# One decoder layer on one core: maxima of the cross attention before the later batches' output and norm, a reciprocal root on VectorE, and weight loads in another place

## What is computed

```
x = x + attn(layernorm(x))            # 16 heads of 64; everything rounded to 1/4096
x = x + xattn(layernorm(x), ctx)      # 16 heads of 8, 1601 keys; mask added to the scores
x = x + ffn(layernorm(x))             # 8 experts, the best 2 per token
```

## Time and profile before

| | |
|---|---|
| median of 3 runs | 681.28 us |
| the profiled execution | 678.65 us |
| its span, first to last instruction | 676.9 us |
| mean granted TensorE clock | 0.933 of full |
| TensorE matmul busy | 565.7 us (84%) |
| VectorE busy | 497.0 us (73%) |
| ScalarE busy | 473.9 us (70%) |
| GpSimd busy | 141.0 us (21%) |

### The profile page before, as it was taken

One profiled execution on the slowest core, in us unless ns is written; L12 is line 12 of the kernel. 1 busy time (PEld: TensorE's weight loads), 2 busy tenths in 40 slices (PEclk: granted clock), 3 DMA queues, 4 the chain that ended last, 5 costly groups with the idle time before them and its releaser, 6 DMA issues.

```text
span 676.9 us, 13952 instructions
## 1 busy us (share of the span) xinstructions
PE 565.7 (84%) x5108; PEld 315.7 (47%) x5115; DVE 497.0 (73%) x896; ACT 473.9 (70%) x850; POOL 141.0 (21%) x215
## 2 busy tenths in 40 slices
PE   5799888988869468999889988999896894799992
PEld 3465555555548233333333333333331242799992
DVE  2578889888986977888878888888884433667662
ACT  3879999998983027778678875878674773577760
POOL 5001001000003433230125011500012106232332
PEclk9999999999999759999999999999996877699995
DMA  9822845723768427010641037000005001111103
GB/s 232 246 103 74 167 166 129 197 83 117 205 174 205 76 98 249 2 51 1 144 126 50 2 67 204 2 1 3 1 1 190 2 1 50 40 41 44 42 28 101
DMA packets 31669, 62.89 MB, mean 93 GB/s; under 512 B 4526, under 2 KB 21338, under 8 KB 31156
## 3 DMA queue, kind: packets, MB, share of 16 engines
q0 software_dynamic: 8000, 40.91, 22.9%
q1 hardware_dynamic: 22020, 20.31, 10.2%
q10 hardware_dynamic: 1584, 0.79, 0.4%
HBM read 42.29 MB, written 19.30 MB: 91 GB/s over the span
## 4 chain that ended last, share of the span: by engine, by line
PE 46%; DVE 20%; ACT 16%; DMA 8%; issue 7%; SPq 1%; POOL 0%; POOLq 0%; ACTq 0%; DVEq 0%
DVE smax L1684 13%; PE pair L1099 11%; PE pair L1074 6%; PE pair L1260 6%; ACT region_p L1340 5%; PE pair L1029 5%; PE pair L1248 3%; ACT region_p L1348 3%; ACT region_p L1438 2%; PE pair L929 2%; DMA region_b<-in_mask_Bx1xSxS_ff 2%; PE pair L916 2%; PE pair L900 2%; PE pair L1270 1%; ACT region_p L1326 1%
## 5 line engine op out<-in xcount | busy, mean ns | idle before, releaser
L1684 DVE TENSOR_REDUCE smax<-pair 128x2 f32<-128x1024 f32 x192 | 225.5, 1219 | 53.5 <-PE pair L1029 52.8
L1438 ACT ACTIVATE region_p<-pair 128x1024 f32<-128x1024 f32 (+3 forms) x277 | 217.7, 812 | 66.8 <-PE pair L1074 61.5
L1557 DVE SCALAR_TENSOR_TENSOR region_p<-region_p 128x1024 int16<-128x1024 int16 (+1 forms) x56 | 67.1, 1220 | 10.3 <-ACT region_p L1326 8.2
L1099 PE MATMUL pair<-region_p 128*32 128x256 f32 (+1 forms) x832 | 69.9, 410 | 0.5 <-ACT region_p L1445 0.4
L1099 PE MATMUL pair<-region_p,region_b 128*32 128x256 f32 (+1 forms) x832 | 66.5, 391 | 0.4 <-ACT region_p L1445 0.4
L1074 PE MATMUL pair<-region_b,region_k 59*128 59x256 bf16 (+1 forms) x416 | 54.7, 273 | 8.7 <-ACT region_p L1438 4.3
L1029 PE MATMUL pair<-region_k,region_b 56*128 56x512 bf16 (+1 forms) x256 | 44.3, 364 | 18.7 <-DVE smax L1684 17.5
L1340 ACT ACTIVATE region_p<-region_p 128x256 f32<-128x256 int16 x128 | 51.4, 413 | 0.0
L916 PE MATMUL pair<-ident,region_p 128*128 128x128 f32 x256 | 36.3, 287 | 11.8 <-DVE region_p L1590 11.8
L1260 PE MATMUL pair<-region_p 128*128 128x128 f32 x368 | 45.5, 277 | 0.0
L929 PE MATMUL pair<-region_p 128*64 128x256 f32 x256 | 34.7, 392 | 12.4 <-ACT region_p L1348 11.5
(11 more groups left out here) (244 smaller groups left out, 970.2 us busy)
## 6 DMA issues: line engine op xcount, KB each, us to landing
kimg<-region_k SPq DMA_DIRECT2D x56, 200.1 KB
region_k<-kimg POOLq DMA_DIRECT2D x8, 1400.9 KB, 18.1
region_b<-in_mask_Bx1xSxS_ff POOLq DMA_DIRECT2D x12, 800.5 KB, 7.6
region_p<-in_mask_Bx1xSxS_ff POOLq DMA_DIRECT2D x4, 800.5 KB, 12.9
region_k<-in_L_ffn_W POOLq DMA_DIRECT2D x3, 1024.0 KB, 9.5
xdisp<-region_x POOLq DMA_DIRECT2D x1, 2322.0 KB, 19.0
region_b<-in_ctx SPq DMA_DIRECT2D x3, 768.0 KB
xdisp<-region_x POOLq DMA_DIRECT2D x1, 2257.5 KB, 18.5
```

What stands on the lines that cost most here:

```text
L1099: last = pe.matmul(pair[3][32 * h:32 * h + 32, 512 + s % 2 * S:512 + (s % 2 + 1) * S], v_heads[b % 2][0:rows, t, c:c + 32], pT[0:rows, n / ...
L1438: act.activation(pT[0:rows, first // 3 % 2, k:k + size], home[0:rows, 0:size], ACT.Exp).then_inc(expt_made, 1)
L1557: return dve.scalar_tensor_tensor(out_, floor16, 0.0, floor16, ALU.is_lt, ALU.add)
L1684: last = dve.tensor_reduce(units[:, :, c // 3, c % 3], both, AX.X, ALU.max)
```

## The change

- **Maxima first.** VectorE no longer outputs and norms tiles 2 to 7 ahead of the maxima. `out_move` only evicts them to 16 bit (`later16`), tiles 2 to 5 before the first pair, 6 and 7 before pair 4. The rest is `out_later(piece)`, six pieces behind pairs 19, 21, 23, 25, 27 and 29, for all six tiles together. TensorE projects tiles 2 and 3, transposes batch 0's queries, projects 4 and 5, and then 6 behind pair 1 and 7 behind pair 2.
- **Lead.** 18 pairs run before event 0 instead of 22; two pairs per event follow until the old schedule is met (`pairs_by`).
- **Queries among scores.** Batches 1, 2 and 3 are transposed in events 30, 50 and 70 in the next free slot of the ring of `pair[0]` and `pair[1]`, and ScalarE copies them after the next event's exponential. The pair that takes the slot next waits for the copy.
- **Root.** The later tiles' norm and the one at event 255 take 1/sqrt by iteration on VectorE, 14 dependent instructions (`norm_root`); the first, second and last norm keep ScalarE's root.
- **GpSimd.** It clamps batch 0's mask and splits maxima 0 and 1 ahead of the later queries. `Wg` and `Wl` are loaded after `split_maxima(7)`. `experts_load` also waits until the shift of group 14 has landed.
- **Branch.** The last batch's `finish_tiles` stand in both branches.
- **Flag.** The reduction of the probe follows `make_attn`, its transposition follows `attn_transposes`.

```diff
+def pairs_by(e):
+    return min(FIRST + 2 * (e + 1), LEAD + 3 * (e + 1) // 4)
 def pairs_at(e):
-    return range(LEAD + 3 * e // 4, LEAD + 3 * (e + 1) // 4)
+    return range(pairs_by(e - 1), pairs_by(e))
...
+QUERIES_AT = (30, 50, 70)
-QUERIES_AT = KT + TAIL_AT
+LATER_AT = (19, 21, 23, 25, 27, 29)
...
# GpSimd
+            for t in range(2):
+                mask_clamp(0, t)
+            split_maxima(0)
+            split_maxima(1)
             pool.wait_ge(proj_mm, len(OUT_TILES))
...
-            pool.wait_ge(xn_made, 1 + len(OUT_TILES))
+            pool.wait_ge(xn_made, 3)
...
-            split_maxima(0)
-            pool.wait_ge(x1_made, len(OUT_TILES))
+            pool.wait_ge(x1_made, 2)
             mask_load(1)
...
+            def gates_load():
+                pool.wait_ge(qstack_made, B)
+                for n, w in enumerate((Wg, Wl)):
...
             def experts_load():
+                pool.wait_ge(shift_loaded, 32 * (GROUPS - 1))
...
             for s in range(1, GROUPS):
-                split_maxima(s)
+                if s > 1:
+                    split_maxima(s)
+                if s == 7:
+                    gates_load()
                 if s == GROUPS - 2:
                     experts_load()
# TensorE
+            project_out(1, (2, 4))
             queries_T(0, pair[0])
-            project_out(2)
+            project_out(1, (4, 6))
...
+                for later in range(1, B):
+                    if n == SLOT["queries", later]:
+                        pe.wait_ge(qstack_made, later + 1)
...
-                for p in range(LEAD):
+                for p in range(FIRST):
                     pair_of_chunks(p, masked)
-                    if p == QUERIES_AT:
-                        for b in range(1, B):
-                            queries_T(b, pair[2 + (b + 1) % 2])
-                pe.wait_ge(qstack_made, B)
+                    if p in (1, 2):
+                        project_out(2, (5 + p, 6 + p))
+                pe.wait_ge(out_moved, 2)
                 burst(st_bank[2])
...
+                        if e in QUERIES_AT:
+                            b = QUERIES_AT.index(e) + 1
+                            pe.wait_ge(slot_done, SLOT["queries", b] - 1)
+                            queries_T(b, pair[SLOT["queries", b] % 2])
...
             with pe.If(flag == 0):
                 cross_attention(False)
+                last_finish()
# VectorE
+            def norm_root(tiles):
+                cut_ = slice(*tiles)
+                root, half, square = rstd[:, cut_], std[:, cut_], meanvar[:, cut_, 1]
+                chain.step(dve.tensor_scalar(half, var_eps[:, cut_], -0.5, None, ALU.mult))
+                chain.step(dve.tensor_scalar(root.bitcast(I32), var_eps[:, cut_].bitcast(I32), 1, None, ALU.logical_shift_right))
+                chain.step(dve.tensor_copy(square, root.bitcast(I32)))
+                chain.step(dve.tensor_scalar(square, square, -1.0, ROOT_MAGIC, ALU.mult, ALU.add))
+                chain.step(dve.tensor_copy(root.bitcast(I32), square))
+                for _ in range(3):
+                    chain.step(dve.tensor_tensor(square, root, root, ALU.mult))
+                    chain.step(dve.tensor_tensor(square, square, half, ALU.mult))
+                    chain.step(dve.scalar_tensor_tensor(root, square, 1.5, root, ALU.add, ALU.mult))
...
+            def out_move(c):
+                first, end = OUT_TILES[c]
+                dve.wait_ge(proj_mm, c + 1)
+                dve.scalar_tensor_tensor(later16[:, first - 2:end - 2, :], ...).then_inc(out_moved, 1)
+            def out_later(piece):
+                # 0 truncate, 1 add x, 2 norm_stats, 3 norm_var, 4 norm_root, 5 norm_apply
...
             attention_out(0)
-            attention_out(1)
-            attention_out(2)
+            out_move(1)
...
-            for p in range(LEAD):
+            for p in range(FIRST):
+                if p == 4:
+                    out_move(2)
                 pair_of_chunks(p)
             for e in range(EVENTS):
                 for p in pairs_at(e):
                     pair_of_chunks(p)
+                    if p in LATER_AT:
+                        out_later(LATER_AT.index(p))
...
                 if e == X2_AT:
-                    layer_norm(5, acc, FFN_TILES[0])
+                    norm_stats(acc, FFN_TILES[0])
+                    chain.step(norm_var(FFN_TILES[0]))
+                    norm_root(FFN_TILES[0])
+                    norm_apply(4, acc, FFN_TILES[0])
```

More of the change, by code:

```diff
@@ L62 @@
 REST = S2 - 3 * CHUNK
-LEAD = 22
+LEAD, FIRST = 22, 18
 TAIL_AT = 4
@@ L102, in slot_table @@
 def slot_table():
-    order = []
+    order, table = [], {}
     def pair_of_chunks(p):
@@ L114, in slot_table @@
             pair_of_chunks(p)
+        if e in QUERIES_AT:
+            table["queries", QUERIES_AT.index(e) + 1] = len(order)
         if finish_at(e):
@@ L117, in slot_table @@
     order += [("finish", B - 1, piece) for piece in range(3)]
-    table = {key: n for n, key in enumerate(order)}
+    table.update({key: n for n, key in enumerate(order)})
     for s in range(GROUPS):
@@ L971, in head_pair, with project_out @@
                         pe.transpose(any_row, mask_any[:, :], ident[:, :]).then_inc(any_T, 1)
-                    attn_transposes(hp, b)
                     if last and b == 2:
-                        project_out(0)
-            def project_out(c):
-                first, end = OUT_TILES[c]
-                pe.wait_ge(o_made, B * (HP - 1) + end // 2)
-                for i, t in enumerate(range(first, end)):
+                        project_out(0, OUT_TILES[0])
+            def project_out(c, tiles):
+                pe.wait_ge(o_made, B * (HP - 1) + (tiles[1] + 1) // 2)
+                for t in range(*tiles):
+                    i = t - OUT_TILES[c][0]
                     for n in range(HP):
@@ L983, in project_out @@
                                          wpT[:, n, :], start=(n == 0), stop=(n == HP - 1))
-                last.then_inc(proj_mm, 1)
+                if tiles[1] == OUT_TILES[c][1]:
+                    last.then_inc(proj_mm, 1)
             for hp in range(HP):
@@ L1202, in biases_T, with last_finish @@
                 last.then_inc(bias_rows_T, 1)
[L1204 to L1208 removed]
+            def last_finish():
+                finish_tiles(B - 1, 0, pair[2])
+                finish_tiles(B - 1, 1, pair[3][:, 0:256])
+                biases_T()
+                finish_tiles(B - 1, 2, pair[3][:, 256:512])
+            pe.wait_ge(flag_made, 1)
+            flag = pe.value_load(mask_flag[0:1, :].bitcast(U32))
+            with pe.If(flag == 0):
+                cross_attention(False)
+                last_finish()
+            with pe.Else():
+                cross_attention(True)
+                last_finish()
+            xn_transposes(5, pair[2], FFN_TILES[1])
             gates(1)
@@ L1407, in queries_move @@
                 act.wait_ge(q_T, b + 1)
-                home = pair[2 + (b + 1) % 2 if b else 0]
+                home = pair[SLOT["queries", b] % 2 if b else 0]
                 act.activation(qstack[b], home[:, :].bitcast(BF16).rearrange("p (h q) -> p h q", h=HP), ACT.Copy).then_inc(qstack_made, 1)
@@ L1421, in _ @@
             queries_move(0)
-            std_of(3, OUT_TILES[1])
-            std_of(4, OUT_TILES[2])
-            for b in range(1, B):
-                queries_move(b)
             act.activation(warm[:, :], var_eps[:, 0:1], ACT.Exp)
@@ L1553, in layer_norm @@
                 last.then_inc(xn_made, 1)
+            def layer_norm(n, root, src, tiles=(0, NT), meanwhile=None):
+                norm_stats(src, tiles)
+                norm_var(tiles).then_inc(var_made, 1)
+                if meanwhile:
+                    meanwhile()
+                dve.wait_ge(std_made, root)
+                chain.step(dve.reciprocal(rstd[:, slice(*tiles)], std[:, slice(*tiles)]))
+                norm_apply(n, src, tiles)
             def truncate(out_, floor16):
@@ L1666, in attention_out @@
                 dve.tensor_copy(rows_of(2), xn_0).then_inc(qnat_made[0], 1)
-                for t in range(2):
-                    dve.wait_ge(mask_loaded[t], 16)
-                    dve.tensor_scalar(masks[0][:, t, :], masks[0][:, t, :], LOWEST, None, ALU.max).then_inc(mclamp_made, 1)
+            def out_move(c):
+                first, end = OUT_TILES[c]
+                dve.wait_ge(proj_mm, c + 1)
+                dve.scalar_tensor_tensor(later16[:, first - 2:end - 2, :], out_home[c].rearrange("p (t d) -> p t d", t=end - first),
+                                         NUDGE, bproj_fx[:, :].unsqueeze(1).broadcast_to([128, end - first, D]),
+                                         ALU.mult, ALU.add).then_inc(out_moved, 1)
+            def out_later(piece):
+                tiles = slice(*LATER)
+                if piece == 0:
+                    dve.wait_ge(out_moved, 2)
+                    chain.step(truncate(xn[:, tiles, :], later16))
```

(15 more changed lines are left out.)

60 lines of the change are left out of this document (24 added, 36 removed).

## The result

The changed kernel takes 690.64 us in the median of 20 runs (682.71 to 707.34), the kernel before 680.49 (676.53 to 685.09, 20 runs). The ratio is 1.0099, 95% interval 1.0069 to 1.0128; the comparison leaves the longest runs out, which is why it is under the ratio of the medians, 1.015. The forecast was 684.2 in a range of 672 to 691. The profiled execution takes 684.10 us, span 680.8, where the sum had given 681.55. So two things need explaining: 2.5 us in the profiled execution, and that the median lies 6.5 above it, with a spread of 25 us where the kernel before has 9. Of the 2.5, 1.5 lie outside the span: 3.3 us here against 1.75. In the changed kernel's 20 runs this share is 1.7 to 3.5 us, in 71 runs of the kernel before 1.7 to 1.8; which edit does it, no run shows. Inside the span the sum is short by 1.0: 3.9 us for 2.9.

The account below looks back on a forecast made before the run. DVE was taken to bound the lead, TensorE the cross attention, DVE and ACT close behind. Terms -1.7 + 2.3 + 4.6 - 7.7 + 10.6 - 5.2 = +2.9 gave 681.55 us profiled, 684.2 median; range 672 to 691.

Parts of the forecast that it names:

- second rival: Query transposes among scores cost all they contain, nothing hidden: 6.5 us more than booked, 690.7 us; chance 0.15.
- step 4: Query transposes at events 30, 50, 70: next pair waits for ACT's copy, 1.9 us each; loss 4.6 us.
- step 3: POOL's order: split of maxima 2 comes late behind query split, mask load and clamp; TensorE waits, loss 2.3 us.
- step 1: Lead: first maximum at 220.5, first exponential about 245.7, 13.3 us earlier, not booked as gain.
- 2. Catch-up: DVE's pairs 18 to 29 and six pieces: pair 30 starts at 269.4 instead of 271.11, gain 1.7 us.
- 5. Expert weights: Loads behind shift 14: TensorE's 6.31 us gap and the half clock behind it go, gain 7.7 us.
- 6. Gate weights: Loads ahead of shift 7: shift lands with them, an 8.3 us gap and half clock behind, loss 10.6 us.
- 7. Tail: Last norm, branch and first block: table switch goes, row transfers limit the gain to about 5.2 of 7.6 us.
- first rival: Shift 7 is not held behind the gate weights: without the 10.6 us, 673.6 us; chance 0.19.
- The third: Rival on the lead: the early start counts in full, 11.6 us better, 672.6 us; chance 0.06.

Follow-up runs that it names:

- run 4: Changed kernel with the second batch's first mask clamp moved behind the split of group 2's maxima; 686.43 us.
- run 5: Changed kernel with GpSimd's two clamps of the first batch's masks held until the first queries are split; 687.76 us, ratio to before 1.0105.
- run 2: Changed kernel without the expert-weight loads' wait for the shift of group 14; 706.16 us.
- run 7: Changed kernel with the first batch's clamps held and queries transposed at events 31, 51 and 67 instead of 30, 50 and 70; 682.99 us.
- run 1: Changed kernel with the gate-weight loads also waiting until shift 7 has landed; 676.48 us, ratio to before 0.9916.
- run 10: Kernel before plus expert weights behind shift 14 and the norm at event 255 with its root by iteration; 672.98 us, ratio 0.9816.
- run 9: Changed kernel with first clamps held, and first masks' and second batch's key loads held until the ones have landed; 688.97 us.
- run 3: Kernel before with only the expert-weight loads' wait for shift 14 added; 672.00 us, ratio 0.9883.
- run 8: Changed kernel with the first batch's clamps held and 22 pairs of chunks ahead of the first scores instead of 18; 684.83 us.
- run 6: Kernel before with only the clamps of the first batch's masks moved from VectorE to GpSimd; 680.29 us, ratio 1.0007.
- run 12: Changed kernel with the mends of run 1, run 4, run 7 and run 9 together; 676.80 us, ratio to before 0.9931.

## Why the prediction was right or wrong

A small loss was forecast and a small loss came: 2.9 us forecast, 3.9 inside the span of the profiled execution, and in the median some 6 us more than forecast, 0.4 under the upper end of the range. That the median is the second rival's 690.7 is chance: that rival put 6.5 us more on the query steps, where the profile has 2.1 more. Within the profile, too, errors cancel: steps 1 to 3 came out 2.5 us better (1.1 of it a self attention that ended earlier), steps 5 and 6 together 3.2 better, stretch 5-6 0.4 better; step 4's stretches and the tail came out 4.2 worse, and 2.9 belong to no step. By its steps, in the profiled execution:

1. Lead: first maximum at 218.97 for 220.5, first exponential at 243.72 for 245.7, of which 1.1 is a self attention that ended earlier. It held for this execution only. What failed is the sentence "The clamps of batch 0 cost POOL 8.5 us while it is free" in step 3, and that step 1 took the start of the transposes, "when DVE has them", as a fixed time. In run 4 T0 lay 5 us later by the clamps alone, in run 5 6 by the late ones alone, in run 2 14 by both. That is enough for the longest runs. What lifts the median by 6.5 us over the profile stays open: these delays are of the size, but holding the clamps moved only the longest runs, and two profiles of fourteen have the ones late. I had asked what hides each edit, not which slack before absorbed the DMAs' lateness: the 8.5 us of output and norm that the change took out of the way.
2. Catch-up: pair 30 starts at 267.01 for 269.4; less those 1.1, a gain of 3.0 where 1.7 was forecast, inside its bounds.
3. GpSimd's order: a wait of 2.08 for the split; by run 4 1.9 for it and 0.8 for the half clock behind it, 2.7 for **2.3**. Right, mechanism and size.
4. Queries: 2.43, 2.61 and 2.47 in the stretches 2-3, 3-4 and 4-5, 7.5 in all; less the 0.8 of step 3, 6.7 for **4.6**. The mechanism is right, the term mis-sized: 2.5 each instead of 1.9. The 1.1 that I took off for shift 2 is there once GpSimd is in time: in run 4 the first of the three costs 1.6. Run 7 shows that the next pair's wait isn't what costs, which leaves ScalarE's copy.
5. Expert weights: 9.0 for **7.7**; right.
6. Gate weights: 8.7 for **10.6**. The mechanism is right (run 1), the size by how it is held: the shift did not wait for the transfer to drain, it took 6.82 us as shift 14 had taken 6.99, and the weights flowed on at 352 GB/s from its landing at 392.42 to 395. I had the number in the earlier trace rows and computed another. The Trainium skill (page "DMA: Bandwidth & Descriptors", section "Queues, rings and completion order") says that the engines take turns between the queues packet by packet; the reading of it in the prediction, a delay of near nothing, is refuted: 6.3 to 6.8 us for shift 7 in seven executions, 7.0 to 7.6 for shift 14 in three, 1.8 for either with the wait.
7. Tail: 4.3 at the first block, 3.9 at the end, for **5.2**, inside its bounds; the row transfers do bound it, as the chain of waits and TensorE's first block show:

```profile
576.52 2.29 DMA xdisp<-region_x,slots
...
579.90 1.84 DMA region_p<-xdisp
```
```profile
581.78 0.48 PE L1267 MATMUL pair<-ident,region_p 128*128 128x128 f32 x1 [2.83 <-DMA region_p<-xdisp]
```

I had not separated its parts, and the runs don't either: in run 10, without the branch's edit, nothing of the root's gain arrived, but in run 9, with it, next to nothing did either, both at a clock of about 0.7. In the sum the tail's gain leans on what TensorE's clock does there.

Not in the sum: 2.9 us behind shift 9 (stretch 9-10). It comes without the change's early parts (run 3, 20.83) and stays away with them (run 8, 18.04), so it isn't the change's alone. But a lowered clock stands there in one of five profiles with the old lead and in seven of nine with the new one; whether the change makes it likelier is open.

The first rival (shift 7 not held) falls by run 1, the third (the early start in full) by run 8. The second priced the query steps at 11.1 net, against 6.7 measured.

## What to carry to other kernels

A wait that keeps a bulk load behind one small transfer on the critical path is the cheapest edit here: one line gave 9 us (run 3), and its absence cost 8.7 (run 1). Before taking work out of the space between an uncertain DMA and the critical engine, ask how late that DMA can be, and look at several executions: one profile shows one landing. An engine that is idle is not free if another, on the critical path, reads and writes SBUF meanwhile.

## What the runs showed of the hardware

A subtraction of 128x256 on VectorE takes 0.43 us alone and 3.36 to 3.48 under GpSimd's clamp, a cast of 0.29 up to 4.24 (run 4), a one-input 128x4 addition 3.47 for 0.17 (run 6); reductions from PSUM are untouched (3.48 us for three, 218.97 in the changed kernel).

A wait of about 2 us for a shift sometimes lowers TensorE's clock and sometimes not, with the same code. Behind shift 9 the granted clock over 10 us is 0.66 in the changed kernel (above); in the kernel before and in run 1 the rows are (the second begins 1.5 us before the wait's end; over the 10 us behind it the clock is 0.83 too):

```profile
422.60:432.60 10.00, 9.63 (x112) 3.27 (x112) 7.56 (x9) 8.06 (x11) 3.98 (x5) 1.00 0.01 2
```
```profile
426.30:436.30 10.00, 8.47 (x84) 2.84 (x84) 6.30 (x7) 5.97 (x9) 4.26 (x1) 0.83 0.05 19
```

At 1.00 stretch 9-10 takes 18.0 to 18.3 us (six of the fourteen profiles), at 0.83 19.5 to 19.7 (two), at 0.66 to 0.69 20.8 to 21.1 (six). The length of the wait parts them, but not quite: at 1.00 TensorE had waited 1.57 to 1.83 us, at 0.83 1.94 and 2.16, at 0.66 to 0.69 1.91 to 2.09 in five profiles and 1.75 in one, where 1.76 in the kernel before lowered nothing. Up to three microseconds between two profiles of this kernel can be this.

SyncE's small store (75 KB each, the last two of four) took 8.4 to 14 us to land: 8.4 and 8.5 with none of GpSimd's loads issued (runs 9 and 12), 9.2 to 9.7 or 13.8 to 13.9 with them, where the landing can be read.
